# Near rows in rounds of four slots through two PSUM buffers, the first round copied by ScalarE and the later ones folded by VectorE

## What is computed

```
mask = adj != 0
scores = where(mask, -arange(N), -inf)
vals, idx = top_k(scores, 25)              # the 25 neighbours with the lowest numbers
feats = x[idx], -inf where not valid
agg = feats.max(axis=2)                    # (8, 2048, 256)
agg = where(degree <= 25, maximum(agg, 0), agg)
h = relu(concat([x, agg]) @ W + b)
out = layernorm(x + h)
```

## Time and profile before

| | |
|---|---|
| median of 3 runs | 2962.48 us (2958.92 to 2973.71) |
| the profiled execution, first to last instruction | 3670.4 us |
| busy: VectorE, TensorE, GpSimd, ScalarE | 2242.2, 2158.4, 1734.9, 1513.4 us |
| near matmuls (L688) | 8880, 1286.3 us |
| reductions of near results (L795) | 384, 848.6 us |
| gathers (L415) | 1664, 1678.7 us |
| combine tree (L903) | 384, 537.8 us |

### The profile page before, as it was taken

One profiled execution on the slowest core, in us unless ns is written; L12 is line 12 of the kernel. 1 busy time (PEld: TensorE's weight loads), 2 busy tenths in 40 slices (PEclk: granted clock), 3 DMA queues, 4 the chain that ended last, 5 costly groups with the idle time before them and its releaser, 6 DMA issues. The chain is left out here.

```text
span 3670.4 us, 49715 instructions
## 1 busy us (share of the span) xinstructions
PE 2158.4 (59%) x15539; PEld 1533.6 (42%) x15664; DVE 2242.2 (61%) x4477; ACT 1513.4 (41%) x3313; POOL 1734.9 (47%) x1860
## 2 busy tenths in 40 slices
PE   2666365536665366656666666635666565666664
PEld 1444244324444244434444444423444444444443
DVE  2566466556676466656666757655766565666664
ACT  5444244323444244434444534423544353444421
POOL 2343544534453544544545444524545554544443
PEclk8788677777888678878887878867888787888887
DMA  4343554434553554544554554533554444544443
GB/s 148 93 126 98 101 113 139 115 75 108 111 150 105 93 123 115 153 111 107 130 134 129 130 116 118 157 76 100 130 124 133 115 132 111 134 113 128 113 85 58
DMA packets 143754, 426.71 MB, mean 116 GB/s; under 512 B 37953, under 2 KB 54850, under 8 KB 126018
## 3 DMA queue, kind: packets, MB, share of 16 engines
q0 software_dynamic: 82176, 224.50, 31.6%
q1 hardware_dynamic: 61250, 198.45, 15.3%
HBM read 405.28 MB, written 16.78 MB: 115 GB/s over the span
## 5 line engine op out<-in xcount | busy, mean ns | idle before, releaser
L415 POOL DMA_INDIRECT got<-in_x,index x1664 | 1678.7, 1009 | 1735.3 <-issue 835.2
L688 PE MATMUL near_ps<-parts,hot 128*128 128x256 bf16 x8880 | 1286.3, 310 | 739.1 <-DVE got L795 577.8
L795 DVE TENSOR_REDUCE got<-near_ps 128x256 f32<-128x2048 f32 (+4 forms) x384 | 848.6, 2210 | 1017.9 <-remote 577.0
L688 PEld LDWEIGHTS near_ps<-parts,hot 128*128 128x128 bf16 x8880 | 965.9, 111 | 1093.1 <-DVE got L795 555.2
L456 ACT ACTIVATE flag<-out_ps 1x1 int32<-1x1 f32 x128 | 20.6, 161 | 1602.5 <-remote 843.3
L903 DVE TENSOR_TENSOR got<-got 128x2048 f32<-128x2048 f32 (+2 forms) x384 | 537.8, 1400 | 14.4 <-DMA got<-in_x,index 4.7
L491 ACT ACTIVATE val<-z_ps,rank_col 128x1024 f16<-128x1024 f32 (+1 forms) x256 | 226.9, 886 | 75.1 <-remote 45.3
L510 ACT ACTIVATE far<-val,beyond 128x128 bf16<-128x128 f16 (+7 forms) x488 | 254.1, 591 | 0.1
L496 ACT ACTIVATE sign<-adj_sb 128x2048 bf16<-128x2048 int32 x128 | 242.9, 1898 | 0.0
L500 ACT ACTIVATE mask_t<-sign 128x2048 bf16<-128x2048 bf16 x128 | 242.7, 1896 | 0.0
L657 PE MATMUL z_ps<-mask_t,local_b 128*128 128x512 bf16 x259 | 110.3, 428 | 193.5 <-ACT val L491 145.9
(11 more groups left out here) (123 smaller groups left out, 2099.5 us busy)
## 6 DMA issues: line engine op xcount, KB each, us to landing
adj_sb<-in_adj_turned SPq DMA_DIRECT2D x128, 1024.0 KB
xx_sb<-in_x_both SPq DMA_DIRECT2D x128, 256.0 KB
got<-in_x,index POOLq DMA_INDIRECT x1664
out<-result SPq DMA_DIRECT2D x128, 128.0 KB
heads<-in_x_near SPq DMA_DIRECT2D x8, 1536.0 KB
hot<-vacant SPq DMA_DIRECT2D x80, 6.0 KB
got_more<-in_x,index_more POOLq DMA_INDIRECT x48, 6.2
w_sb<-in_L_gnn_W SPq DMA_DIRECT2D x1, 512.0 KB
```

Source lines behind the costliest of these rows:

```text
L415: pool.indirect_dma_start(out=to, out_offset=None, in_=x_rows, in_offset=bass.IndirectOffsetOnAxis(ap=at, axis=0)).then_inc(landed, 16)
L688: mm = pe.matmul(near_ps[:, s - k * ROUND:s - k * ROUND + 1, :], hot[:, a.i, s * P:(s + 1) * P], parts[:, (a.side * PARTS + n) * CH + c, N ...
L795: dve.tensor_reduce(got[:, a.i, FAR + k, :], near_ps[:, 0:n, :].rearrange("p q c -> p c q"), AX.X, ALU.max).then_inc(near_used, 1)
```

## The change

A round is now four slots, two PSUM banks, and `near_ps` has two such buffers, used in turn through the whole program (`buffer_of`); it is as large as before. A tile has five rounds (19 slots) or six. ScalarE copies round 0 into the four near places of `got`; VectorE folds every later round into these four places with an elementwise maximum, each fold waiting for the one before it. `near_used` is replaced by `near_copied` (ScalarE) and `near_taken` (VectorE); TensorE fills a buffer again when its last use has been copied or folded. The combine starts from 13 + 4 rows in place of 13 + 3. The order of the work is written anew in the `step` of TensorE, VectorE and ScalarE; SyncE's wait for `near_used` becomes one for `near_taken`.

```diff
-ROUND = 8
+ROUND = 4
+BUFFERS = 2
...
-        got = sb("got", [P, 2, FAR + NR, C], F32)
+        got = sb("got", [P, 2, FAR + ROUND, C], F32)
...
-        near_ps = ps("near_ps", [P, ROUND, C], F32)
+        near_ps = ps("near_ps", [P, BUFFERS, ROUND, C], F32)
...
+        def taken(g, t, k):
+
+            return g * TAKEN_SUM + (ROUND_AT[t] - t + k + BASE)
+
+        def buffer_of(a, k):
+
+            return (a.side * ROUND_SUM + ROUND_AT[a.t] + k) % BUFFERS
...
-                        sp.wait_ge(near_used, rounds_done(b.g, b.t, ROUNDS[b.t] - 1))
+                        sp.wait_ge(near_taken, taken(b.g, b.t, ROUNDS[b.t] - 1))
...
+            def copy_first_round(a):
+                act.wait_ge(near_ready, rounds_done(a.g, a.t, 0))
+                act.wait_ge(agg_ready, done(a.T - 2))
+                act.activation(got[:, a.i, FAR:FAR + ROUND, :], near_ps[:, buffer_of(a, 0), :, :],
+                               ACT.Copy).then_inc(near_copied, 1)
...
+                if a1.there:
+                    copy_first_round(a1)
                 if a2.there or a5.there:
                     act.wait_ge(small_in_ps, done(a5.T))
...
-                pe.wait_ge(near_used, rounds_done(a.g, a.t, k - 1))
+                if k == BUFFERS:
+                    pe.wait_ge(near_copied, done(a.T))
+                else:
+                    pe.wait_ge(near_taken, taken(a.g, a.t, k - BUFFERS if k > BUFFERS else k + 1 - BUFFERS))
...
-                    near(a1, 1)
+                    near(a1, 2)
+                    near(a1, 3)
...
-                    near(a1, 2)
+                    near(a1, 4)
+                    near(a1, 5)
                 if a2.there:
                     near(a2, 0)
+                    near(a2, 1)
...
-            def reduce_near(a, k):
+            def take_near(a, k):
...
-                dve.tensor_reduce(got[:, a.i, FAR + k, :], near_ps[:, 0:n, :].rearrange("p q c -> p c q"), AX.X,
-                                  ALU.max).then_inc(near_used, 1)
+                if k == 1:
+                    dve.wait_ge(near_copied, done(a.T))
+                else:
+                    dve.wait_ge(near_taken, taken(a.g, a.t, k - 1))
+                dve.tensor_tensor(got[:, a.i, FAR:FAR + n, :], near_ps[:, buffer_of(a, k), 0:n, :],
+                                  got[:, a.i, FAR:FAR + n, :], ALU.max).then_inc(near_taken, 1)
...
-                rows = FAR + ROUNDS[a.t]
+                rows = FAR + ROUND
...
-                def third():
+                def fifth():
                     if a1.there:
-                        reduce_near(a1, 2)
+                        take_near(a1, 4)
...
                 if a1.there:
-                    reduce_near(a1, 0)
+                    take_near(a1, 1)
                 if a0.there:
                     combine(a0)
                 if last.there:
                     invert(last)
                 if a1.there:
-                    reduce_near(a1, 1)
+                    take_near(a1, 2)
+                    take_near(a1, 3)
                 if a2.there:
                     mark_cells(a2)
                 if a3.there:
-                    find(a3, inner, third)
+                    find(a3, inner, fifth)
...
+                if a1.there:
+                    take_near(a1, 5)
```

More of the change, by code:

```diff
@@ L66, in build @@
     NR = max(ROUNDS)
+    TAKEN_SUM = ROUND_SUM - PG
     CH = max(len(p) for p in PLAN)
@@ L75, in build @@
     assert FAR < KEPT == 2 * WORD and x_near.shape[2] == CH and HOTS <= P // 4
-    assert CH + 2 < PG - 1 and 2 <= min(ROUNDS) and NR <= 3 and FIRST < CH <= FIRST + BANK // P
+    assert CH + 2 < PG - 1 and 2 + BUFFERS <= min(ROUNDS) and NR <= 6 and min(NEAR) >= ROUND and FIRST < CH <= FIRST + BANK // P
     x_rows = x.rearrange("b n c -> (b n) c")
@@ L225, in build @@
         near_ready = sem("near_ready")
-        near_used = sem("near_used")
+        near_copied = sem("near_copied")
+        near_taken = sem("near_taken")
         agg_ready = sem("agg_ready")
@@ L561, in step @@
             def step(pair, u):
-                a0, a2, a3, a4, a5 = (Tile(pair, u, k) for k in (0, 2, 3, 4, 5))
+                a0, a1, a2, a3, a4, a5 = (Tile(pair, u, k) for k in range(6))
                 last, next = Tile(pair, u, -1), Tile(pair, u, LEAD)
+                if a1.there:
+                    copy_first_round(a1)
                 if a2.there or a5.there:
@@ L607, in _ @@
             for count in (sign_ready, mask_ready, counts_ready, limit_ready, flag_ready, above_ready, low_ready,
-                          rest_ready, unfilled_ready, vacant_ready, val_ready, far_ready, numbered_ready, at_moved, mean_ready,
+                          rest_ready, unfilled_ready, vacant_ready, val_ready, far_ready, numbered_ready, near_copied,
+                          at_moved, mean_ready,
                           spread_ready, std_ready, shift_ready, result_ready, hi_ready, mid_ready, lo_ready):
@@ L687, in near @@
                     for n in range(PARTS):
-                        mm = pe.matmul(near_ps[:, s - k * ROUND:s - k * ROUND + 1, :],
+                        mm = pe.matmul(near_ps[:, buffer_of(a, k), s - k * ROUND:s - k * ROUND + 1, :],
                                        hot[:, a.i, s * P:(s + 1) * P],
@@ L881, in combine @@
                 dve.sem_inc(flag_by_vec, 1)
-                dve.wait_ge(near_used, rounds_done(a.g, a.t, ROUNDS[a.t] - 1))
+                dve.wait_ge(near_taken, taken(a.g, a.t, ROUNDS[a.t] - 1))
                 for s in range(FAR - UNDER_WAY, FAR):
@@ L959, in step @@
                 if a3.there:
-                    find(a3, inner, third)
+                    find(a3, inner, fifth)
                 else:
-                    third()
+                    fifth()
                     for take in inner:
                         take()
+                if a1.there:
+                    take_near(a1, 5)
                 if a0.t % 4 == 0:
                     restart()
-            for count in (hot_ready, key_ready, over_ready, index_ready, flag_by_vec, near_used, agg_ready,
+            for count in (hot_ready, key_ready, over_ready, index_ready, flag_by_vec, near_taken, agg_ready,
                           y_ready, rstd_ready, rest_of_hi, rest_of_mid):
```

## The result

The changed kernel takes 2941.53 us in the median of 4 runs (2938.85 to 2946.86), the kernel before 2968.1 us in the median of its 4 runs: a ratio of 0.9915 (95% interval 0.9890 to 0.9939). On a second chip the ratio was 0.9927 (0.9907 to 0.9946). So the change makes the kernel faster by 0.8%, some 25 us, which is clear of the noise but small, where 187 us (6.3%) were forecast. The time lies well outside the forecast's own 2670 to 2830. It lies inside the whole range only because the upper end, 2950, was set to take in the second rival and a part of the third. That third rival, "gathers set the pace already", put at 0.10 and 2950 to 2975 us, is nearest.

The account below looks back on a forecast made before the run. The prediction took VectorE's own work at full clock, plus its waits for TensorE's near matmuls, lengthened by the lower clock, as the bound: 2962.5 - 43 (VectorE work) - 173 (waits) + 25 (gathers) = 2771, rounded to 2775 us; range 2670 to 2950.

Parts of the forecast that it names:

- second rival: TensorE to VectorE: round 1 meets the low clock in nearly every step; the penalty moves but stays, 2830 to 2940 us, chance 0.20.
- third rival: GpSimd: a tile's gathers already take 22 us, so shortening VectorE gives nothing; 2950 to 2975 us, chance 0.10.
- VectorE's sum: VectorE's work: folds for reductions 96 us less, a fourth combine operation 53 us more, net 43 us less.
- The wait for near matmuls after the change: VectorE before round 1's fold: 1.07 us exposed plus 0.62 for the clock, 1.69 us a tile, 216 us in all.
- a sign against it: VectorE before rounds 4 and 5: waits that stay there would mean TensorE's chain is longer than the forecast had it.
- the step on GpSimd: GpSimd's gathers come close to the shortened 20.6 us step; a quicker combine sometimes meets late rows, 25 us added.
- The first reason given against the rival: GpSimd waited 685.7 us for the combine, 11.8 us in each of 58 starts, so it had room.
- The second reason: GpSimd: a tile's gathers need only 16.0 us without late or stretched ones, 13 x 0.95 + 12 x 0.30.
- 389 against 216, 173 us less: VectorE's wait for near matmuls falls from 389 to 216 us; bounds 252 and 42 us less.
- if the combine waits for gathers: Sign at VectorE's combine: if it waits for gathered rows in the changed kernel's profile, the forecast is wrong.
- The granted clock: TensorE: shorter bursts with stops keep the clock low and lose the gain; at 70% half clock 3140 us, chance 0.14.
- Round 1 meets the low clock and passes its lateness on: The second rival's claim: lateness passes into counts, ranks and layer; waits fall only 42 us, giving 2878 us, chance 0.20.

Follow-up runs that it names:

- nine gathers: Kernels before and after, each with four of a tile's thirteen gathers left out: before 2765.61 us (0.9213), after 2640.34 us (0.8790 of the full kernel before).
- the second profile: The kernel before, unchanged, profiled once more on another chip: it spans 3004.7 us, against 3006.3 us for the unprofiled runs there.

## Why the prediction was wrong

**What held.** VectorE's sum: reductions to folds was -96 us and measured -97.4, the combine's fourth maximum +53 and +55.5 (nine gathers). ScalarE's copy takes 130.9 us, 1.02 each, behind 440.5 us of idle time, and VectorE waits 1.8 us for it in all. The wait for near matmuls after the change was to be 1.69 us a tile, 216 us, and is 210.5. That sum is in part luck, since the wait sits otherwise: read off the trace of after in order of time, 147 us of idle time stand before the fold of round 1, 1.15 a tile, where 1.07 at full clock and 0.62 for the clock were forecast, 63 before round 4, where the prediction had none at full clock and named a wait that stays as a sign against it, and under 7 before each of the others.

**What failed first: the step on GpSimd.** "The gathers come close to that" and +25 us. The gathers were the bound already. The combine's wait for them, which the 25 us stood for, is 289.2 us after the change, and was 186.4 before it in the second profile. The first reason given against the rival, 685.7 us in which GpSimd waited for the combine, was read from an execution 24% longer than the runs; in an undisturbed profile the same line has 10.4 us. I had seen that the profile was long, took 577.0 us of VectorE's waits out as a cost of being profiled, which the second profile bears out, and did not ask what these stalls did to the other waits: an engine that is held up lets those ahead of it look idle. The second reason, a floor of 16.0 us a tile from gathers of 0.95 us, left out what is not in an instruction's duration: the landing, with four under way. Rows 8 themselves had 19.4 us a tile, and that was in an execution that gave them time: its mean over all tiles is 18.5, that of the second profile 20.7. Four gathers at 0.95 + 0.30 us each are issued in 5.0 us, so a gather that lands later than 5.0 us after its start holds up the fourth after it. By the semaphore events in the trace of after 31% do (half of all land within 4.3 us), and GpSimd's waits there are 446 in 1664. Six are issued in 7.5 us and eight in 10.0: with six under way 23% land later than 7.5 us, with eight under way 0.1% later than 10.0.

**What failed second: the size of the wait before.** The term "389 against 216, 173 us less" started from the same execution. The undisturbed profile has 345.8 us, and 304.3 with nine gathers. With nine the idle time before the near lines falls by 100 us, not 173. The error is on the side of before: the 216 us after are 195.4 with nine. So without the bound of the gathers the forecast would still have been 60 us too good, and the gain 4.5% and not 6.3%.

**What followed.** VectorE's shorter step ran into the gathers and was given back as a wait at the combine: its idle time there is 304.2 us after, against 196.2 in the second profile of before, a chip 1% slower. The prediction's last paragraph names this sign ("if the combine waits for gathers"). Another of its signs, that GpSimd's wait for the combine goes down, was met without its reason: that wait is 10.4 us in the second profile of before. What the 25 us that were gained consist of is not shown.

**The other rivals.** The granted clock did fall with the change: on the second chip it was 0.862 to 0.871 in the runs of before and 0.829 to 0.837 in those of after. It did not take the time back. VectorE's wait for near matmuls is 210.5 us at 0.835 and 195.4 at 0.898 (nine gathers), so by this estimate the lower clock is worth some 15 us there; the kernel with one more fold has a higher clock than after on the same chip (0.846 against 0.835 in the profiled executions) and is 21 us slower. And the distance is nearly gone once the gathers are relieved, 0.899 to 0.898 with nine and 0.892 to 0.882 with eight under way in the profiled executions. Why it is wider with four is not shown. "Round 1 meets the low clock and passes its lateness on" would have left the wait 42 us under that of before, 347 us in the prediction's terms and 304 by the second profile; it is 210.5. What the Trainium skill tells of a kernel in which two PSUM buffers gave no further gain (page "TensorE: Matmul & The Clock Gate", section "HAM oscillation — how this bites in real kernels") fits the outcome, but not for a cause on TensorE: the same two buffers give 4.5% once the gathers are nearly out of the way.

## What to carry to other kernels

Before reading waits off a profile, hold its span against the timed runs: where it is a quarter longer, every slack and every wait in it is in doubt, not only the odd one, and a second profile comes first. An engine that is busy 63% of the time can be the bound if it may have only a fixed number of DMAs under way; price it by the landings as well as by its instructions, and try the number. An extra piece of work on an engine, with and without the suspected bound, tells quickly whether saving work there can pay.

## What was unexpected of the hardware

- Gathers are stretched where VectorE reads two inputs from SBUF. In the trace of the kernel with the extra operation from SBUF, the 232 gathers that overlap it by over 0.2 us take 1143 ns on average, 105 of them more than 1.1 us; the 229 that overlap the one from PSUM in the other kernel take 945, none of them more than 0.96 us. The Trainium skill has this (page "SBUF — State Buffer", section "Who interferes with whom": a VectorE instruction with two SBUF inputs contends with a GpSimd instruction that reads SBUF), and the trace agrees.
- The end of a gather's instruction says little of its landing: 0.95 us busy, but with four under way a gather starts every (1791.2 + 1011.2) / 1664 = 1.68 us in the kernel after and waits for landings in 446 cases. The Trainium skill, page "Perfetto Trace Analysis", section "DMA Instruction — SWDGE (GPSIMD)", says that the recorded end is when the descriptors have been generated, not when the data have moved; these waits agree.
- One profiled execution of the kernel before was 708 us longer than its runs, with 577.0 us of VectorE waiting for events that the trace ties to no instruction; a second one on another chip had none of it. The first also lacks 125 of the 384 matmuls of the ranks (L657) that the second has. Its cause is not settled.
